# A two-layer graph kernel whose first phase goes by columns, with the diagonal block kept in SBUF and its natural tiles summed by two engines

## The chip, the cores and the metric

The kernel runs on one core of one Trainium2 chip. TensorE multiplies, VectorE and ScalarE work on tiles, GpSimd and SyncE start transfers. Time is the device time of one execution in microseconds (us). The kernel before takes 2062.57 us, the median of three runs between 2061.89 and 2065.29.

## The reference

The input `adj` is a dense 8192 x 8192 float32 matrix (268 MB), and `x` is 8192 x 128. Two graph layers follow each other, each with a product by the whole matrix:

```python
def _L0_gnn_ref(X, adj, W, b):
    adj_hat = adj + jnp.eye(adj.shape[0], dtype=adj.dtype)
    d_inv_sqrt = 1.0 / jnp.sqrt(jnp.sum(adj_hat, axis=1))
    adj_norm = adj_hat * d_inv_sqrt[:, None] * d_inv_sqrt[None, :]
    return jax.nn.relu(adj_norm @ (X @ W) + b)

def _L1_gnn_ref(x, adj, weight, self_weight):
    support = x @ weight
    output = jax.nn.relu(support + adj @ support + x @ self_weight)
    return pair_norm(output)      # over all rows
...
x = _layernorm(x + _L0_gnn_ref(x, adj, L0_gnn_W, L0_gnn_b), axis=-1)
x = _layernorm(x + _L1_gnn_ref(x, adj, L1_gnn_weight, L1_gnn_self_weight), axis=-1)
```

So the first layer needs the row sums of the matrix before it can scale anything: column block c of the product can be used only once the sums of row block c are known. The second layer needs the finished first layer in the same way.

## The kernel before

**Tiles.** The matrix is cut into 8 x 8 blocks of 1024 x 1024. A block is loaded as four tiles of 1 MB (128 partitions x 2048, two slices of 1024 columns), either transposed (`adjT`, ready for the product) or natural (`adjN`, for row sums). Four buffers `raw0` to `raw3` form a ring: SyncE's queue loads the next tile as soon as the tile four places back is consumed.

**A multiplied tile.** ScalarE rounds each slice to `hi` (L371), VectorE forms the rest `lo` (L622), and the same is done for the small factor (`rhi` L365, `rlo` L619). TensorE then makes `hi*rhi + lo*rhi + hi*rlo` for two halves of 512 columns: 6 matmuls a slice, 12 a tile (L1001). When a tile serves both layers at once it is 24, called a dual tile here. There are four buffers each for `hi` and `lo`, which is two tiles: ScalarE can start a slice only when TensorE has done the slice four back.

**Phase 1, by rows.** Row block 0 is 32 natural tiles that VectorE sums (L628). Row block k of 1 to 7 needs the sums of all its eight blocks. Its k blocks left of the diagonal come as `adjT`, are multiplied for layer 0, and their sums are made on TensorE with a matrix of ones (L1007, 4 matmuls a slice). The other 8 - k blocks come as `adjN` for VectorE. Natural tiles are put between multiplied ones as long as there are any (a "pair"), so late rows have multiplied tiles alone. There VectorE adds up three of the eight slices of a block (L718), and TensorE sums the other five. After a row `own_sums`, `lower_sums`, `degree` and `make_z` produce `zr`, the scaled factor of the next column. The phase has 256 tiles, 112 of them multiplied.

**Phase 2** walks the rows from 7 to 0: the diagonal block for layer 0, then the blocks right of it for both layers at once (dual tiles). Since rows are finished from below, layer 1 already has its factor `s1` for those columns. After each row an update of the finished row (transposes, bias, relu, layer norm, the products by `w1` and `wsum`, L774 to L813 and L1072 to L1097) is woven into the next row's tiles. Phase 2 has 144 tiles. **Phase 3** does layer 1 for the diagonal and the blocks left of it, 144 tiles. Then a tail computes the pair norm and the last layer norm and stores the result.

**Accumulators.** Layer 0 has the banks `acc0`, layer 1 the banks `acc1`. At each new row TensorE first waits until VectorE or ScalarE has read the bank, and opens it with a small product by zero (L1015).

All engines run hardware loops (`Fori`) with a register for the row. The programs of the engines are in order: an instruction that waits holds all behind it.

The lines that set the ring and the split:

```python
sp.wait_ge(slice_split, n + (o + 1 - Q) * JB)
sp.dma_start(raw[o % Q][:, :], src[k, c, q]).then_inc(loaded[o % Q], 16)
...
def pair_lo(k, i):
    for q in range(Q):
        lo_of_pair(k, i, q)
        sum_of_pair(k, i, q)
```

Of the kernel before, what the change touches and what calls it, by code (L numbers as in the profile page):

```python
# [3 lines left out]


def graph_kernel(nc, x, xT, adjT, adjN, W0, b_rows, W1, Wself, out):
# [5 lines left out]
    ds = bass.ds  # L39
# [6 lines left out]
    NB = N // BLK  # L46
    Q = 4
    JB = BLK // Q // P
    TILE = JB * BLK
    H = BLK // 512  # L50
    HALF = 512
    G = HALF // P
    EPS_LN = 1e-5
    EPS_PN = 1e-6
    assert NB >= 8 and NB % 2 == 0 and JB == 2 and H == 2

    S = Q * JB  # L60
    LOWER = NB * (NB - 1) // 2
    UPPER = NB * (NB + 1) // 2
    N2 = NB * NB * S
    N3 = N2 + UPPER * S
    SKIP = N2 - (LOWER + 1) * S

    def n1(k, c):
        return k * (NB * S) + c * S

    def n1_pair(k, i):  # L70
        return k * (NB * S) + i * (2 * S)

    def n1_rest(k, i):
        return k * ((NB - 2) * S) + i * S + 2 * NB * S

    def u1(k, c):
        return (k * (k - 1)) * (S // 2) + c * S + S

    def u1_rest(k, i):
        return (k * (k - 3)) * (S // 2) + i * S + (NB + 1) * S  # L80

    def within(v):
        return v if isinstance(v, int) else v.with_bounds(min_val=0, max_val=NB - 1)

    def phase1_rows(eng, row):

        row(1, "first")
        with eng.Fori(2, NB // 2) as k:
            row(k, "few")
        row(NB // 2, "half")  # L90
        with eng.Fori(NB // 2 + 1, NB - 1) as k:
            row(k, "many")
        row(NB - 1, "last")

    def phase1_blocks(eng, k, kind, first_pair, pair, natural, lower, after_lower=None):


        first_pair(k)
        if kind in ("few", "half", "many"):
            with eng.Fori(1, {"few": k, "half": NB // 2, "many": k * -1 + NB}[kind]) as i:  # L100
                pair(k, i)
        if kind in ("first", "few") and natural:
            with eng.Fori(k * 2, NB) as c:
                natural(k, c)
        if kind in ("many", "last"):
            with eng.Fori(0, k * 2 - NB) as i:
                lower(k, i)
            if after_lower:
                after_lower()

    def summed_on_dve(q, j):


        return j == 0 and q < Q - 1

    def n2(m, i):
        return (m * (m + 1)) * (S // 2) + i * S + N2

    def n3(m, i):
        return i * S + N3 if isinstance(m, int) and m == 0 else (m * (m - 1)) * (S // 2) + i * S + (N3 + NB * S)  # L120

# [12 lines left out]

    def k3(m):
        return NB - 1 if isinstance(m, int) and m == 0 else m - 1

    def col3(m, i):
        return i * -1 + (NB - 1) if isinstance(m, int) and m == 0 else i

    ctx = ExitStack()
    with ctx:
# [9 lines left out]


# [4 lines left out]

        raw = [sb(f"raw{q}", [P, TILE]) for q in range(Q)]

        hi = [sb(f"hi{r}", [P, BLK], f32r) for r in range(2 * JB)]
        lo = [sb(f"lo{r}", [P, BLK], f32r) for r in range(2 * JB)]


        rhi = [[sb(f"rhi{r}{l}", [P, JB * P], f32r) for l in range(2)] for r in range(2)]
        rlo = [[sb(f"rlo{r}{l}", [P, JB * P], f32r) for l in range(2)] for r in range(2)]

# [6 lines left out]
        rows = sb("rows", [P, P])  # L174
        d = sb("d", [P, N // P])
        rsum = sb("rsum", [P, NB * BLK // P])
        deg = sb("deg", [P, BLK // P])
        sq = sb("sq", [P, BLK // P])
        nw = sb("nw", [P, BLK // P])
        low = sb("low", [P, BLK // P])  # L180
        onesr = sb("onesr", [P, P], f32r)
        st = sb("st", [P, G, 6])
        ost = w0[:, 0:H * NB * 6]
        mean = sb("mean", [P, G])
        mv = sb("mv", [P, 2])
# [22 lines left out]
        ones_set = sem("ones_set")  # L208
# [4 lines left out]
        banks_free = sem("banks_free")  # L213
# [15 lines left out]
        upd_step = sem("upd_step")
# [1019 lines left out]
```

## Time and profile before

| | us |
|---|---|
| three runs | 2062.57, 2065.29, 2061.89 |
| profiled execution, first to last instruction | 2063.7 |
| TensorE busy | 1724.0 (84%) |
| VectorE busy | 1694.2 (82%) |
| ScalarE busy | 1063.7 (52%) |
| tiles loaded | 544, 570 MB |

The profiled execution is the one that the rows below come from. An engine's busy time is the time in which it executes; what lies between is idle time, with the instruction or transfer that ended it (the releaser). Matmuls overlap in the pipeline, so a single one lasts longer (0.39 us) than the distance between two of them; the distance is what counts for a sum. The page also gives the granted clock of TensorE in tenths of full speed. PEld is TensorE's weight load, which overlaps its matmuls.

### The profile page before, as it was taken

The page shows a single profiled execution, that of the slowest core. Times are in us where ns is not written, and L with a number is a line of the kernel's source. Part 1 is how long each engine was busy: PE and PEld are TensorE (multiplying, and loading weights), DVE is VectorE, ACT ScalarE, POOL GpSimd, SP SyncE. Part 2 cuts the span into 40 slices and gives each one's busy share as a digit, 9 for nine tenths or more (in the row PEclk, how much of TensorE's full clock was granted, in tenths as well). Part 3 has the DMA queues.
Part 4 walks back from the last instruction along what each step waited for, and adds up shares of the span by engine and source line. Part 5 has one row for each costly group of instructions (what it writes and reads, how often), then busy time and mean ns, then how long its engine had stood idle before and what let it go on. Part 6 is the DMA issues. An engine that isn't in the chain of part 4 may idle for free.

```text
span 2063.7 us, 26085 instructions
## 1 busy us (share of the span) xinstructions
PE 1724.0 (84%) x7538; PEld 1393.6 (68%) x7538; DVE 1694.2 (82%) x2195; ACT 1063.7 (52%) x1496; POOL 21.4 (1%) x34
## 2 busy tenths in 40 slices
PE   1134374989999997799999999999999999999993
PEld 1023263767777786677788887887887777787772
DVE  7989998999898996688675857658557999999996
ACT  0102132344545564455555545445445688888875
POOL 0000000000000100000000000000000000000001
PEclk9966787999999998899999999999999999999995
DMA  9999999999797985355555545455455699999972
GB/s 391 394 404 381 408 381 389 362 367 380 277 348 261 331 320 191 138 201 214 187 190 196 211 183 218 174 197 208 179 202 224 266 365 352 359 369 366 357 291 82
DMA packets 81956, 583.74 MB, mean 283 GB/s; under 512 B 9152, under 2 KB 9152, under 8 KB 12288
## 3 DMA queue, kind: packets, MB, share of 16 engines
q1 hardware_dynamic: 78336, 570.46, 71.7%
q0 software_dynamic: 3584, 12.85, 1.9%
q8 instruction: 17, 0.28, 0.1%
q14 instruction: 19, 0.16, 0.0%
HBM read 579.08 MB, written 4.19 MB: 283 GB/s over the span
## 4 chain that ended last, share of the span: by engine, by line
PE 60%; DVE 18%; DMA 13%; issue 5%; ACT 2%; DVEq 1%; POOL 0%; ACTq 0%; SPq 0%; POOLq 0%
PE acc L1001 54%; DVE lo L622 7%; DMA raw<-in_adjN 7%; DMA raw<-in_adjT 6%; DVE rsum L628 5%; PE acc L1007 3%; ACT hi L371 2%; DVE rlo L619 1%; PE pC L1096 1%; PE pD L1097 1%; PE acc L1015 0%; DVE t L678 0%; DVE o L898 0%; DVE s L953 0%; DMA rows<-in_b_rows 0%
## 5 line engine op out<-in xcount | busy, mean ns | idle before, releaser
L371 ACT ACTIVATE hi<-raw 128x1024 fp32r<-128x1024 f32 x800 | 821.5, 1054 | 417.8 <-DMA raw<-in_adjT 304.9
L622 DVE TENSOR_TENSOR lo<-raw,hi 128x1024 fp32r<-128x1024 f32 x800 | 943.3, 1220 | 7.1 <-ACT hi L371 7.1
L1001 PE MATMUL acc<-hi,rhi 128*128 128x512 f32 x2048 | 825.3, 403 | 122.4 <-DVE lo L622 121.5
L1001 PE MATMUL acc<-lo,rhi 128*128 128x512 f32 x2048 | 806.9, 394 | 0.0
L1001 PE MATMUL acc<-hi,rlo 128*128 128x512 f32 x2048 | 639.9, 394 | 0.0
L1001 PEld LDWEIGHTS acc<-hi,rhi 128*128 128x128 f32 x2048 | 389.8, 190 | 228.6 <-DVE lo L622 146.0
L1001 PEld LDWEIGHTS acc<-hi,rlo 128*128 128x128 f32 x2048 | 389.5, 190 | 83.8
L1001 PEld LDWEIGHTS acc<-lo,rhi 128*128 128x128 f32 x2048 | 390.1, 190 | 81.4 <-issue 3.3
L628 DVE TENSOR_REDUCE rsum<-raw 128x2048 f32 (+1 forms) x144 | 328.0, 2282 | 19.7 <-DMA raw<-in_adjN 18.5
L619 DVE TENSOR_TENSOR rlo<-zr,rhi 128x256 fp32r<-128x256 f32 x256 | 108.3, 423 | 231.3 <-ACT hi L371 229.5
L365 ACT ACTIVATE rhi<-zr 128x256 fp32r (+1 forms) x256 | 105.1, 411 | 308.5 <-PE acc L1001 297.9
L1015 PE MATMUL acc<-zero,ident 128*128 128x2 f32 x148 | 24.6, 272 | 155.4 <-ACT ux L391 124.5
L1007 PE MATMUL acc<-hi,onesr 128*128 128x512 f32 x376 | 152.1, 405 | 0.0
L1007 PE MATMUL acc<-lo,onesr 128*128 128x512 f32 x376 | 151.1, 402 | 0.0
L1015 PEld LDWEIGHTS acc<-zero,ident 128*128 128x128 f32 x148 | 23.4, 222 | 165.7 <-ACT ux L391 126.9
L619 DVE TENSOR_TENSOR rlo<-s,rhi 128x256 fp32r<-128x256 f32 x256 | 107.8, 421 | 13.2 <-ACT hi L371 11.8
L365 ACT ACTIVATE rhi<-s 128x256 fp32r (+1 forms) x256 | 102.7, 401 | 4.2 <-PE acc L1001 4.2
L1007 PEld LDWEIGHTS acc<-lo,onesr 128*128 128x128 f32 x376 | 73.1, 194 | 17.3
L1007 PEld LDWEIGHTS acc<-hi,onesr 128*128 128x128 f32 x376 | 72.5, 193 | 17.3
L376 ACT ACTIVATE sq<-deg 128x8 f32<-128x8 f32 x8 | 1.7, 209 | 126.8 <-DVE rsum L656 126.8
L718 DVE TENSOR_TENSOR o<-o,raw 128x1024 f32<-128x1024 f32 x36 | 44.1, 1225 | 2.7 <-DMA raw<-in_adjT 0.8
L813 DVE TENSOR_TENSOR o<-o,pD 128x512 f32 (+1 forms) x16 | 10.9, 682 | 26.9 <-PE pD L1097 26.9
(116 smaller groups left out, 508.2 us busy)
## 6 DMA issues: line engine op xcount, KB each, us to landing
raw<-in_adjT SPq DMA_DIRECT2D x400, 1024.0 KB, 4.9
raw<-in_adjN SPq DMA_DIRECT2D x144, 1024.0 KB, 7.4
o<-in_xT POOLq DMA_DIRECT2D x8, 512.0 KB, 8.7
s<-in_x POOLq DMA_DIRECT2D x8, 512.0 KB, 17.8
out<-zr POOLq DMA_DIRECT2D x8, 512.0 KB, 4.6
w<-in_W POOLq DMA_DIRECT2D x2, 64.0 KB, 6.1
t<-in_Wself POOLq DMA_DIRECT2D x1, 64.0 KB, 6.3
rows<-in_b_rows POOLq DMA_DIRECT2D x1, 64.0 KB, 7.0
```

What stands on the lines that cost most here:

```text
L365: nc.scalar.activation(rhi[q % 2][q // 2 if single else l][:, :], src[:, ds(c * BLK + q * JB * P, JB * P)], ACT.Copy)
L371: nc.scalar.activation(hi[q % 2 * JB + j][:, :], raw[o % Q][:, j * BLK:(j + 1) * BLK], ACT.Copy).then_inc(hi_ready, 1)
L619: V.tensor_sub(rlo[q % 2][p][:, :], src[:, ds(c * BLK + q * JB * P, JB * P)], rhi[q % 2][p][:, :].bitcast(f32))
L622: V.tensor_sub(lo[r][:, :], raw[o % Q][:, j * BLK:(j + 1) * BLK], hi[r][:, :].bitcast(f32)).then_inc(slice_split, 1)
L628: V.tensor_reduce(rsum[:, ds(c * (BLK // P) + q * JB, JB)], raw[o % Q][:, :].rearrange("p (g j) -> p g j", g=JB), AX.X, ALU.add).then_inc( ...
L718: V.tensor_add(colsum, colsum, raw[q][:, j * BLK:(j + 1) * BLK])
L813: V.tensor_add(half(o1, k, h), half(o1, k, h), pD[:, :]).then_inc(self_added, 1)
L1001: last = T.matmul(banks[h][:, :], stat[:, j * P:j * P + P], mov[:, h * HALF:(h + 1) * HALF], start=False, stop=(end and stat is rlo[q % 2] ...
L1007: last = T.matmul(acc1[h][:, :], onesr[:, :], mov[:, h * HALF:(h + 1) * HALF], start=False, stop=(end and mov is l_), skip_group_check=True)
L1015: T.matmul(bank[:, 0:2], ident[:, :], zero[:, 0:2], start=True, stop=False, skip_group_check=True)
L1096: T.matmul(pC[:, j * P:j * P + P], t2[:, j * P:j * P + P], w1[:, :], start=True, stop=True)
L1097: T.matmul(pD[:, :], wsum[:, :], t2[:, :], start=True, stop=True).then_inc(s1_made, 1)
```

## The change

The kernel is written anew around a list of tiles ("chunks") that all engines walk in the same order, without hardware loops. What is computed stays the same.

- **Phase 1 goes by columns.** Stage 0 loads the diagonal block (0,0) as `adjT` into four tiles of its own in `o1` ("keep"), and the natural tiles of row 0 right of the diagonal. Stage k of 1 to 7 multiplies column k-1: first the diagonal block (k-1,k-1) from SBUF ("cached", no transfer), then all blocks (i,k-1) below it. Beside them, one after each product tile, come the natural tiles of row k right of the diagonal and the diagonal block (k,k). No block left of the diagonal is loaded as natural, and no diagonal block as natural.
- **Sums.** Natural tiles of even q are summed on ScalarE (a copy with `accum_out`), those of odd q on VectorE (L606). The kept block is added up on VectorE into `colsum` (one `tensor_add` of two slices, then six of 128 x 1024). The sums of multiplied blocks below the diagonal are made on TensorE with `pick`, a matrix whose one column of ones puts them into row i of `pC` and `pD`. At the end of a stage `close_sums`, `read_sums`, `turn_degree` and `degree` bring the parts of one row together.
- **More work in phase 1, less after it.** Layer 0 of the diagonal blocks 0 to 6 and of block (5,6) is now done in phase 1. Phase 2 keeps (7,7), (4,5), (6,7) for layer 0, (7,7) for layer 1, and 25 dual blocks. Phase 3 has 38 blocks. The tiles loaded are 112 natural, 32 kept and 380 multiplied, 524 in all.
- **Partial results.** Each column visit to a row block ends after one block, and VectorE adds the accumulator to `ux` (L659, two of 128 x 512). Single-layer visits alternate between two sets of banks; the first matmul of a visit has `start=True`, and the small opening products are gone.

```diff
+    for k in range(NB):
+        sums, products = [], []
+        for c in range(k + 1, NB):
+            for q in range(Q):
+                sums.append(Chunk("sum", k, c, q, act=(q % 2 == 0), stage=k))
+        kept = [Chunk("keep", k, k, q, stage=k) for q in range(Q)]
+        if k == 0:
+            chunks += kept + sums
+            continue
+        sums[Q:Q] = kept
+        multiply_block(products, k - 1, k - 1, (L0,), new_visit(k - 1, (L0,), 1, [k - 1], first=(k == 1)),
+                       cached=True, stage=k)
+        for i in range(k, NB):
+            multiply_block(products, i, k - 1, (L0,), new_visit(i, (L0,), 1, [k - 1], first=(k == 1)),
+                           summed=True, stage=k)
+        if k == NB - 1:
+            multiply_block(products, 5, 6, (L0,), new_visit(5, (L0,), 1, [6]), stage=k)
+        for n, chunk in enumerate(products):
+            chunk.tail = n - (len(products) - Q)
+            chunks.append(chunk)
+            if n < len(sums):
+                chunks.append(sums[n])
...
+    add_visit(NB - 1, (L0,), 2, [NB - 1], cached=True, final=True)
+    add_visit(4, (L0,), 2, [5])
+    add_visit(6, (L0,), 2, [7], final=True)
+    add_visit(7, (L1,), 2, [7])
+    add_visit(5, (L0, L1), 2, [7], final=True)
+    add_visit(4, (L0, L1), 2, [7, 6], final=True)
+    for k in (3, 2, 1, 0):
+        add_visit(k, (L0, L1), 2, list(range(NB - 1, k, -1)), final=True)
+    add_visit(7, (L1,), 3, [6, 5, 4, 3, 2, 1, 0], last=True)
+    for k in (0, 1, 2, 3):
+        add_visit(k, (L1,), 3, list(range(k, -1, -1)), last=True)
...
+            for chunk in chunks:
+                if chunk.kind == "keep":
+                    if chunk.row > 0:
+                        sp.wait_ge(slice_split, kept_end[chunk.row - 1, chunk.q])
+                    sp.dma_start(kept[:, chunk.q * TILE:(chunk.q + 1) * TILE],
+                                 adjT[chunk.row, chunk.col, chunk.q]).then_inc(kept_in[chunk.q], 16)
+                elif chunk.ring >= 0:
+                    if chunk.ring >= RAW:
+                        by, count = ring_chunks[chunk.ring - RAW].freed
+                        sp.wait_ge(raw_free[by], count)
...
+            def sum_rows(chunk):                      # ScalarE
+                act.wait_ge(*landed(chunk))
+                for j in range(JB):
+                    g = chunk.col * BG + chunk.q * JB + j
+                    ins = S.activation(slice_of(chunk, j), slice_of(chunk, j), ACT.Copy,
+                                       accum_out=rsum[chunk.row % 2][:, g:g + 1])
+                ins.then_inc(act_summed, 1)
...
+            def add_visit_up(v):                      # VectorE
+                dve.wait_ge(slice_multiplied, v.end)
+                for h in range(H):
+                    u, a = half(ux, v.row, h), acc[v.sets[L0]][h][:, :]
+                    ins = V.tensor_copy(u, a) if v.first else V.tensor_add(u, u, a)
+                ins.then_inc(l0_read, 1)
...
+            for n, chunk in enumerate(mul_chunks):    # TensorE
+                multiply(chunk)
+                after_rows(n)
+                if chunk.stage > 0 and chunk.tail == 0:
+                    close_sums(chunk.stage)
+                if chunk.stage > 0 and chunk.tail == 1:
+                    turn_degree(chunk.stage)
+                if chunk.stage > 0 and chunk.tail == 2:
+                    first_product(chunk.stage)
```

VectorE's program in a row of pairs before (L619 and L622 split a multiplied tile, L628 sums a natural one), and then in the middle of a stage of the changed kernel (L598 and L600 split, L606 sums, L659 adds a visit to `ux`). Before:

```order
L619 ISA [waits hi_ready]
L619 TENSOR_TENSOR rlo<-zr,rhi 128x256
L622 TENSOR_TENSOR lo<-raw,hi 128x1024
L615 REGISTER_ALU
L622 TENSOR_TENSOR lo<-raw,hi 128x1024 [waits hi_ready]
L627 ISA
L628 ISA [waits loaded1]
L628 TENSOR_REDUCE rsum<-raw 128x2
L615 REGISTER_ALU
L619 ISA [waits hi_ready]
L619 TENSOR_TENSOR rlo<-zr,rhi 128x256
L622 TENSOR_TENSOR lo<-raw,hi 128x1024
```

And changed:

```order
L598 TENSOR_TENSOR rlo<-zr,rhi 128x256 [waits hi_ready]
L600 TENSOR_TENSOR lo<-raw,hi 128x1024
L600 TENSOR_TENSOR lo<-raw,hi 128x1024 [waits hi_ready]
L598 TENSOR_TENSOR rlo<-zr,rhi 128x256 [waits hi_ready]
L600 TENSOR_TENSOR lo<-raw,hi 128x1024
L600 TENSOR_TENSOR lo<-raw,hi 128x1024 [waits hi_ready]
L659 TENSOR_TENSOR ux<-ux,acc 128x512 [waits slice_multiplied]
L659 TENSOR_TENSOR ux<-ux,acc 128x512
L606 TENSOR_REDUCE s<-raw 128x2 [waits loaded3]
```

Two tiles are split for one that is summed; the other natural tile is ScalarE's, and the visit's addition stands between.

VectorE at the start of stage 7, where the stage has no natural tiles. The cached tiles of block (6,6), read from `o`, are split, and each is followed by the additions of a tile of block (7,7), which goes to the same place in `o` (L616 and L620):

```order
L598 TENSOR_TENSOR rlo<-zr,rhi 128x256 [waits hi_ready]
L600 TENSOR_TENSOR lo<-o,hi 128x1024
L600 TENSOR_TENSOR lo<-o,hi 128x1024 [waits hi_ready]
L616 TENSOR_TENSOR s<-o 128x1024 [waits sums_closed,kept_in0]
L598 TENSOR_TENSOR rlo<-zr,rhi 128x256 [waits hi_ready]
L600 TENSOR_TENSOR lo<-o,hi 128x1024
L600 TENSOR_TENSOR lo<-o,hi 128x1024 [waits hi_ready]
L659 TENSOR_TENSOR ux<-ux,acc 128x512 [waits slice_multiplied]
L659 TENSOR_TENSOR ux<-ux,acc 128x512
L620 TENSOR_TENSOR s<-s,o 128x1024 [waits col_step,kept_in1]
L620 TENSOR_TENSOR s<-s,o 128x1024 [waits col_step]
```

In the stages before, four natural tiles stand in these places and the additions come with the next four product tiles.

SyncE's queue from stage 6's kept tiles to stage 7's (L369 loads a kept tile of 1 MB, L376 a tile into the ring):

```order
L376 DMA raw<-in_adjT 128x2048 [waits act_summed]
L369 DMA o<-in_adjT 128x2048 [waits slice_split]
L376 DMA raw<-in_adjT 128x2048 [waits dve_summed]
L369 DMA o<-in_adjT 128x2048 [waits slice_split]
L376 DMA raw<-in_adjT 128x2048 [waits act_summed]
L369 DMA o<-in_adjT 128x2048 [waits slice_split]
L376 DMA raw<-in_adjT 128x2048 [waits dve_summed]
L369 DMA o<-in_adjT 128x2048 [waits slice_split]
L376 DMA raw<-in_adjT 128x2048 [waits slice_split] x4
L369 DMA o<-in_adjT 128x2048 [waits slice_split] x4
L376 DMA raw<-in_adjT 128x2048 [waits slice_split] x272
```

In stage 6 the loads of kept tiles take turns with product tiles. In stage 7 four of them follow each other, each behind the split of the tile whose place it takes, and all later tiles stand behind them.

## Rows read from the trace of the kernel before

**Rows 1.** Windows by phase: length, busy us of each engine, granted clock, DMA, GB/s.

```profile
0.00:797.50 797.50, 539.89 (x2296) 429.95 (x2296) 710.82 (x636) 276.52 (x364) 14.27 (x26) 0.90 0.90 353
797.50:1576.30 778.80, 756.59 (x3380) 616.34 (x3380) 534.03 (x910) 399.95 (x618) 0.00 (x0) 0.99 0.52 194
1576.30:2008.60 432.30, 411.86 (x1797) 335.31 (x1796) 411.37 (x509) 357.64 (x454) 0.00 (x0) 0.98 0.87 340
2008.60:2063.70 55.10, 15.67 (x66) 11.98 (x66) 37.95 (x142) 29.57 (x61) 7.08 (x8) 0.57 0.27 76
```

**Rows 2.** The page: TensorE's clock in 40 slices, and the queues that fetch instructions.

```profile
PEclk9966787999999998899999999999999999999995
...
q8 instruction: 17, 0.28, 0.1%
q14 instruction: 19, 0.16, 0.0%
```

**Rows 3.** Groups by line and shape: count, busy us, mean ns, idle before.

```profile
L622 DVE TENSOR_TENSOR lo<-raw,hi 128x1024 fp32r<-128x1024 f32 x800 | 943.3, 1220 | 7.1 <-ACT hi L371 7.1
L371 ACT ACTIVATE hi<-raw 128x1024 fp32r<-128x1024 f32 x800 | 821.5, 1054 | 417.8 <-DMA raw<-in_adjT 304.9 <-PE acc L1007 62.4 <-PE acc L1001 49.4
L628 DVE TENSOR_REDUCE rsum<-raw 128x2048 f32 x128 | 291.8, 2283 | 19.6 <-DMA raw<-in_adjN 18.5 <-issue 0.4
L718 DVE TENSOR_TENSOR o<-o,raw 128x1024 f32<-128x1024 f32 x36 | 44.1, 1225 | 2.7 <-DMA raw<-in_adjT 0.8
L1015 PE MATMUL acc<-zero,ident 128*128 128x2 f32 x148 | 24.6, 272 | 155.4 <-ACT ux L391 124.5 <-DVE t L678 11.2 <-DVE o L898 10.9
L1045 PE MATMUL acc<-o,onesr 128*128 128x512 f32 x12 | 5.6, 592 | 0.0
```

**Rows 4.** VectorE's timeline in row 0, natural tiles alone: start, length, idle before.

```profile
85.73 2.29 DVE L628 TENSOR_REDUCE rsum<-raw 128x2048 f32 x1 [0.20 <-DMA raw<-in_adjN]
```

**Rows 5.** VectorE's timeline in pairs: early in row 1, then in row 4.

```profile
100.13 0.41 DVE L619 TENSOR_TENSOR rlo<-zr,rhi 128x256 fp32r<-128x256 f32 x1
...
102.73 2.28 DVE L628 TENSOR_REDUCE rsum<-raw 128x2 f32<-128x2048 f32 x1
104.93 0.41 DVE L619 TENSOR_TENSOR rlo<-zr,rhi 128x256 fp32r<-128x256 f32 x1
```

```profile
424.45 0.43 DVE L619 TENSOR_TENSOR rlo<-zr,rhi 128x256 fp32r<-128x256 f32 x1 [0.51 <-ACT hi L371]
...
429.81 0.42 DVE L619 TENSOR_TENSOR rlo<-zr,rhi 128x256 fp32r<-128x256 f32 x1 [0.47 <-ACT hi L371]
```

**Rows 6.** The chain that ended last, TensorE: start, length, matmuls.

```profile
739.93 2.73 PE acc L1001 x12
...
755.55 2.73 PE acc L1001 x12
...
1462.04 114.30 PE acc L1001 x504
1577.71 2.84 PE acc L1001 x12
...
1863.12 65.46 PE acc L1001 x288
1930.67 77.94 PE acc L1001 x336
```

**Rows 7.** The tile raw on the load queue: time from issue to landing.

```profile
DMA to landing us min/median/max: 4.6/4.9/13.3
```

**Rows 8.** TensorE in two stretches of phase 1: busy us, granted clock, DMA, GB/s.

```profile
150.00:165.00 15.00, 0.00 (x0) 0.50 1.01 424
375.00:390.00 15.00, 14.88 (x72) 1.00 0.89 336
```

**Rows 9.** VectorE's timeline in one half of a row's update, phase 3.

```profile
1593.14 0.69 DVE L774 TENSOR_TENSOR pA<-pA,zr 128x512 f32<-128x512 f32 x1
...
1602.66 0.41 DVE L619 TENSOR_TENSOR rlo<-s,rhi 128x256 fp32r<-128x256 f32 x1
```

More of the change, by code:

```diff
@@ L30 @@
 from contextlib import ExitStack
+from dataclasses import dataclass, field
+@dataclass
+class Chunk:
+    kind: str
+    row: int
+    col: int
+    q: int
+    layers: tuple = ()
+    cached: bool = False
+    act: bool = False
+    summed: bool = False
+    stage: int = -1
+    tail: int = -1
+    ring: int = -1
+    freed: tuple = ()
+    base: int = -1
+    stats: tuple = ()
+    visit: int = -1
+@dataclass
+class Visit:
+    row: int
+    layers: tuple
+    phase: int
+    cols: list
+    final: bool = False
+    first: bool = False
+    last: bool = False
+    out: int = -1
+    end: int = -1
+    sets: dict = field(default_factory=dict)
+    waits: dict = field(default_factory=dict)
+    done: int = -1
 def graph_kernel(nc, x, xT, adjT, adjN, W0, b_rows, W1, Wself, out):
@@ L70, in n1_pair @@
[L70 to L109, printed above, removed]
@@ new lines, in graph_kernel @@
+    ORDER = {row: m for m, row in enumerate(FINAL_ROWS)}
+    done = [(c.layers[l], c.row, c.col, c.q) for c in chunks if c.kind == "mul" for l in range(len(c.layers))]
+    assert len(done) == len(set(done)) == 2 * NB * NB * Q
+    ring = slices = stats = act_sums = dve_sums = 0
+    for chunk in chunks:
+        if chunk.kind == "mul":
+            chunk.base = slices
+            slices += JB
+            chunk.stats = tuple(range(stats, stats + len(chunk.layers)))
+            stats += len(chunk.layers)
+            chunk.freed = ("split", slices)
+            visits[chunk.visit].end = slices
+        elif chunk.kind == "sum" and chunk.act:
+            act_sums += 1
+            chunk.freed = ("act", act_sums)
+        elif chunk.kind == "sum":
+            dve_sums += 1
+            chunk.freed = ("dve", dve_sums)
+        if chunk.kind != "keep" and not chunk.cached:
+            chunk.ring = ring
+            ring += 1
@@ L141, in graph_kernel, with since_last @@
+    def since_last(n):
+        for at in range(n - 1, -1, -1):
+            v = mul_chunks[at].visit
+            if last_chunk[v] == at and visits[v].last:
+                return visits[v], n - 1 - at
+        return None, -1
     ctx = ExitStack()
@@ L355, in _ @@
         def _(act):
[L356 to L372 removed]
+            S = nc.scalar
@@ L571, in _ @@
             act.wait_ge(ln_ready, 1)
-            with act.Fori(BATCH + 2, NB - 1) as k:
+            for k in range(BATCH + 2, NB - 1):
                 pair_norm(k)
@@ L578, in _ @@
             last_root(1)
-            with act.Fori(2, BATCH) as k:
+            for k in range(2, BATCH):
                 last_norm(k)
```

1103 lines of the change are left out of this document (464 added, 639 removed).

## The prediction, made before the changed kernel ran

> **What bounds the kernel now.** I read the windows by phase first, then the chain that ended last, then VectorE's timeline inside phase 1, and the groups by line for prices. The windows [rows 1] show phase 1 with 797.5 us, phase 2 with 778.8, phase 3 with 432.3 and a tail of 55.1. In phase 2 TensorE is busy for 756.6 of 778.8 us at a clock of 0.99, and VectorE and the transfers have room: it is TensorE's. The chain confirms this: 504 matmuls in 114.30 us without a break, 0.227 us each [rows 6]. So a multiplied tile costs TensorE 12 x 0.227 = 2.72 us, a dual tile 5.44, and a tile with sums (20 matmuls) 4.55. In phase 3 all three are close: TensorE 411.9, VectorE 411.4 of 432.3 us, and 24 tiles take 65.46 us, 2.73 each, in the inside of a row [rows 1, 6]. In phase 1 TensorE is busy 540 us and VectorE 711 of 797 us, transfers run at 0.90. Its early rows wait for tiles and VectorE, its late rows for TensorE: a block without natural tiles takes 755.55 - 739.93 = 15.6 us [rows 6], which is its 68 matmuls back to back. So phase 1 leaves some 250 us of TensorE idle while phase 2 has none to spare. Work moved from phase 2 into these gaps is the change's one large effect.
>
> **Prices.** VectorE's split of a tile: 102.73 - 100.13 = 2.60 us, and a natural tile 104.93 - 102.73 = 2.20, up to 2.28 [rows 3, 5]. Adding a slice of a kept tile: 1.225 [rows 3], 9.0 us for the seven of a block with their handovers. Transfers: one tile in 2.29 + 0.20 = 2.49 us where only sums are made [rows 4], and (429.81 - 424.45)/2 = 2.68 in late pairs, where VectorE waits 0.5 us for a tile [rows 5]. Half an update on VectorE: 1602.66 - 1593.14 less the one split inside, 6.9 us [rows 9]; with two additions of half a slice I take 16.5 us for a whole update. A visit's addition to `ux` is not in the trace; the nearest is an addition from a bank at 0.69 [rows 9], so 1.4 us for two; it can hardly be below 1.2 or above 1.5. TensorE's own part of an update: 756.6 us busy less 3072 products at 0.227 (697) less 30 openings at two records of 0.17 leaves 50 us for seven updates [rows 1, 3], some of it at the lower clock; I take 6.6 us each.
>
> **Stage 0.** 32 tiles as before, but eight are in flight at the start, not four, and ScalarE takes half of the sums. VectorE's 0.2 us waits per tile are for transfers [rows 4], so the rate stays at 2.49. The last tile is summed at about 85.5, then `degree`, the root, and `first_product`, which now waits for the degree. That makes `zr` ready at 91 and VectorE's first split at 92. Before it was at 95: nearly nothing gained.
>
> **Stages 1 to 6** have three parts.
> - *Four cached tiles with four natural ones, then four product tiles with the kept block.* VectorE: 8 x 2.60 + 2 x 2.28 + 9.0 + 2 x 1.4 = 37.2 us. TensorE needs 4 x 2.72 + 4 x 4.55 = 29.1, transfers 12 x 2.49 = 30. VectorE is the bound.
> - *6 - k groups of four product tiles with four natural ones.* TensorE 18.2 us, VectorE 4 x 2.60 + 2 x 2.28 + 1.4 = 16.4, transfers 8 x 2.6 = 20.8. For a tile I take 2.6 between 2.49 and 2.68, since holding times in the ring fall with VectorE's relief. The ring is full at the start of this part, which gives some 8 us of lead: 96, 75, 55, 36, 18 and 0 us for k of 1 to 6, together 280.
> - *The last four product tiles and the chain to the next `zr`.* TensorE finishes two tiles (9.1) and `close_sums`, four records of 0.47 us [rows 3], 1.9. Then `turn_degree`: 16 records, 2.5 us by the small opening products at 0.17 [rows 3]. Then a tile and `first_product` follow, 6.9 us. VectorE's chain (root, `hi` at 1.05, the split of the last tile, five small steps) is done in about the same time. Two multiplications into `zr`, `rhi` and the next `hi` follow. From the start of this part to VectorE's next split: 22.5 us.
>
> Six times 37.2 + 22.5 is 358, with 280 it is 639 us.
>
> **Stage 7** has no natural tiles, so the kept loads of (7,7) come beside the cached tiles of (6,6), into the same places. VectorE splits tile q, only then its load is issued, it lands after at least 4.6, mostly 4.9 us [rows 7], and VectorE stands before the addition with tile q+1 behind it. That is 2.6 + 4.9 + 2.45 four times over (the first with one addition), 39 us where VectorE's own work is 20.8. With 2.6 us to the first product, 18.2 for four tiles, 2 for a clock that fell meanwhile, and 18.5 for the last part: 80 us. Phase 1 ends at 92 + 639 + 80 = 811, later than before (797.5), though it does 8 blocks more, worth 8 x 4 x 2.72 = 87 us of TensorE.
>
> **Phase 2.** (7,7) and then eight single tiles carry row 7's update: VectorE 11.8 + 8 x 2.60 + 16.5 + 1.4, and TensorE ends 52.5 us after the start. Four tiles of (7,7) for layer 1 and four dual ones carry row 6's update. The single ones are paced by VectorE and the dual ones by TensorE: 49. Eight dual tiles of row 4 with row 5's update: 43.5 + 6.6 and a bank wait of 1.6, 51.7. Rows 3 to 0: 88 dual tiles 479, four updates 26.4, four bank waits 6.4, 512. The bank wait is priced by 1577.71 less 1462.04 + 114.30, 1.4 us [rows 6]. Together 665 us against 778.8: ten block products fewer are 109 of these 114 us.
>
> **Phase 3.** 152 tiles x 2.73 = 415, TensorE's part of row 0's update 6.6. That update falls on 8 single tiles instead of 12, where VectorE has 20.8 + 16.5 us, so 10 us are lost. Before, each of seven row changes cost 1930.67 - 1863.12 - 65.46 = 2.1 us [rows 6]. Now two sets of banks take turns, but VectorE has 2.8 us of extra work (two additions, two statistics) and only 0.12 us of slack per tile, so I keep 1.8. With the first bank wait of 1.6: 446 us, 14 more than before for 8 tiles more.
>
> **The tail** does the same steps; without registers and loops I take 52 for 55.1 us. **Sum:** 811 + 665 + 446 + 52 = 1974 us as the profile would count it. The profiled 2063.7 us stand 1.1 us above the median 2062.57, so 1973 us, 4.3% less.
>
> **The rivals.** (A) *The handovers in phase 1 cost more than the largest engine's work.* For: late pairs lose 0.5 us per tile pair for a tile [rows 5], and in all of phase 1 VectorE is busy only 711 of 797 us [rows 1]. If the groups run at 2.68 a tile with no lead, they take 15 x 21.4 = 321 instead of 280. With 5% on the other parts of stages 1 to 6 (18 us) the time is 2032. Against: at 100 us, with tiles in store, VectorE ran 4.80 us per pair without idling [rows 5].
>
> (B) *The engines overlap better.* The starts of the last parts hide under VectorE's lead, the lead in the ring carries over, and phase 3 loses nothing at row changes: 18 in phase 1, 10 in phase 3, some 1945 us.
>
> (C) *Fetching instructions, slower than before.* The trace shows 36 fetches in all [rows 2]. The program before lists some 6400 instructions, weight loads counted, so one fetch brings about 180; the loops then run from what is there. The straight-line program has some 14900 on TensorE alone (7457 matmuls with their weight loads), some 80 fetches. If each stops TensorE for a landing of 4.6 us [rows 7], that is 370 us: 2340. The kernel becomes slower than before from 89/80 = 1.1 us a fetch. Against it: one fetch lasts TensorE more than 20 us (90 matmuls of 0.227), and a request made that early can queue behind several tiles and still be in time. The Trainium skill, page "Runtime: NRT & Kernel Launch", section "Instruction fetch mechanics", says that the next block is fetched while the current one runs, mostly hidden, and that a taken branch out of the window stalls. By this rule the new code should not pay and the loops before should. For loops the trace shows no such price: the 504 matmuls without a break in rows 6 run through them.
>
> (D) *TensorE's clock.* With TensorE idle the clock is at 0.50 (1.2 GHz), with 14.88 of 15 us busy at 1.00 [rows 8], and phase 1 had a mean of 0.90 [rows 1]. New stages have it busier (some 600 of 720 us), so the clock should be up. Were it at 1.2 GHz for a quarter of the 400 us of stages that TensorE paces, 50 us: 2023. To become slower than before it would need almost half of them.
>
> **How the numbers follow.** Forecast 0.57, A 0.24, B 0.09, C 0.06, D 0.04. The predicted time is the forecast's, 1973. Its own bounds: visit additions, `turn_degree` and the clock after stage 7 give plus or minus 15, the lead 8, updates in phases 2 and 3 plus or minus 12. The range takes in B and most of A: 1940 to 2038. This kernel's measurement can tell about 0.2% from no change. Faster by more than that (below 2058.4) are the forecast, B, nearly all of A and half of D: 0.91. Within 0.2%, the edge of A and D: 0.03. Slower, from C and a bad D: 0.06.
>
> **What would show it.** Phase 2 should start near 811 us and run to 1476, TensorE at over 95% in its rows. In stages 1 to 6 VectorE should be without idle at the start and TensorE in the last four tiles. Stage 7 should show four waits of some 5 us before the additions to `colsum`. Stage boundaries near 248, 383, 497, 593, 671 and 731 show the terms apart. A phase 1 that ends beyond 850, TensorE idle with "issue" as the reason at even distances (C), or a clock of 0.5 within busy stages (D) would make the prediction wrong.

## The result, and the profile after

The changed kernel takes 2025.11 us (median of four runs, 2023.29 to 2030.02) against 2062.24 us for the kernel before on the same chip: a ratio of 0.982, 95% interval 0.9803 to 0.9837. It is faster, by 1.8%, where 4.3% were forecast. The time lies inside the range, but less than half of the forecast gain came.

The windows by phase of the changed kernel (columns as in [rows 1]; the first is stage 0, the second stages 1 to 7):

```profile
0.00:93.80 93.80, 11.11 (x36) 8.15 (x36) 43.68 (x33) 35.72 (x64) 4.08 (x12) 1.00 0.99 410
93.80:854.50 760.70, 679.18 (x2876) 530.37 (x2876) 591.95 (x657) 432.78 (x623) 7.04 (x11) 0.97 0.82 320
854.50:1523.60 669.10, 639.03 (x2844) 520.70 (x2844) 458.61 (x822) 329.66 (x516) 3.16 (x4) 0.98 0.51 183
1523.60:1967.60 444.00, 428.50 (x1860) 347.07 (x1860) 430.95 (x534) 373.48 (x477) 0.00 (x0) 0.99 0.91 350
1967.60:2022.30 54.70, 16.25 (x66) 12.91 (x66) 37.79 (x143) 29.57 (x61) 7.20 (x8) 0.52 0.27 77
```

| part | before [rows 1] | forecast | after |
|---|---|---|---|
| phase 1 | 797.5 | 811 | 854.5 |
| phase 2 | 778.8 | 665 | 669.1 |
| phase 3 | 432.3 | 446 | 444.0 |
| tail | 55.1 | 52 | 54.7 |
| profiled execution | 2063.7 | 1974 | 2022.3 |

43.5 us of the miss of 48 are in phase 1. To find the stage, VectorE's timeline is read at each stage's first split, the row behind the last multiplication into `zr`. Stage 1 begins with the first of these rows, phase 2 with the last:

```profile
93.85 0.43 DVE L598 TENSOR_TENSOR rlo<-zr,rhi 128x256 fp32r<-128x256 f32 x1 [1.43 <-ACT hi L439]
...
854.47 0.43 DVE L598 TENSOR_TENSOR rlo<-zr,rhi 128x256 fp32r<-128x256 f32 x1 [1.43 <-ACT hi L439]
```

| stage | 1 | 2 | 3 | 4 | 5 | 6 | 7 |
|---|---|---|---|---|---|---|---|
| forecast length, us | 155.7 | 134.7 | 114.7 | 95.7 | 77.7 | 59.7 | 80 |
| measured | 166.8 | 145.5 | 124.0 | 105.0 | 79.5 | 60.8 | 79.1 |
| over | 11.1 | 10.8 | 9.3 | 9.3 | 1.8 | 1.1 | -0.9 |

Stage 6 has no middle group and was right within 1.1 us, and stage 7 too. In stage 6 VectorE is done with the kept block at 752.27, so the first part took 37.6 us and the last 23.1. The fixed parts of a stage (37.2 and 22.5 us) were right, and what is over belongs to the middle groups. VectorE adds a visit to `ux` once in each group, so the distance between these rows is a group. From stage 1:

```profile
135.49 1.28 DVE L659 COPY ux<-acc 128x512 f32<-128x512 f32 x2
136.69 2.28 DVE L606 TENSOR_REDUCE s<-raw 128x2 f32<-128x2048 f32 x1
...
143.73 0.42 DVE L598 TENSOR_TENSOR rlo<-zr,rhi 128x256 fp32r<-128x256 f32 x1 [2.16 <-ACT hi L439]
...
155.06 0.43 DVE L598 TENSOR_TENSOR rlo<-zr,rhi 128x256 fp32r<-128x256 f32 x1 [2.27 <-ACT hi L439]
...
157.67 1.28 DVE L659 COPY ux<-acc 128x512 f32<-128x512 f32 x2
```

This group takes 22.2 us. In stages 1 to 4 ten groups can be read so, and they take 21.0 to 24.2. The last group of each stage reads shorter (18.2 to 20.0), since its visit is added when the product tiles without natural ones have begun. Over all 15 groups the stages leave 21.6 each (below). The first is no faster than the next ones. VectorE waits some 2 us for `hi` at most of the product tiles shown. At 155.06 ScalarE had a natural tile's sum ahead of it, but ScalarE's own waits are for tiles, as its timeline in the same place shows:

```profile
158.93 2.01 ACT L439 ACTIVATE hi<-raw 128x1024 fp32r<-128x1024 f32 x2 [2.65 <-DMA raw<-in_adjT]
161.46 1.06 ACT L445 ACTIVATE raw<-raw 128x1024 f32<-128x1024 f32 x1 [0.53 <-DMA raw<-in_adjN]
```

The time from issue to landing of the ring's tiles, over the whole kernel, to be set against [rows 7] (4.9); then in the groups of stage 1 (issues from 135 to 240 us); then in late pairs before (400 to 500 us):

```profile
DMA to landing us min/median/max: 4.6/6.1/20.5
```

```profile
DMA to landing us min/median/max: 5.1/7.5/10.3
```

```profile
DMA to landing us min/median/max: 5.0/6.9/8.3
```

So transfers were late, at 21.6/8 = 2.7 us a tile, though in stage 0 they come at 2.49 (a tile of 1.05 MB at 422 GB/s):

```profile
20.00:80.00 60.00, 6.55 (x20) 4.16 (x18) 27.43 (x12) 27.22 (x50) 0.00 (x0) 1.00 1.01 422
```

Two theories can explain that. **R**: the ring of four places is too short. A place is held from landing until the engine that reads the tile last is done with it, then the next transfer needs its time, and this cycle of 4 x 2.7 = 10.8 us over four places sets the rate. **M**: the memory path gives no more while three engines work. The other loss that phase 1 shows is stage 7's waits, forecast and seen.

### The profile page after: what moved, and what is told of

Same layout as the page of the kernel before. It is cut to its first block, busy times and chain, and to the rows that moved or that the text cites. A ratio compares the mean times of both kernels' runs of the same rounds, so it can differ in the third digit from the quotient of the medians.

```text
span 2022.3 us, 21035 instructions
## 1 busy us (share of the span) xinstructions
PE 1774.1 (88%) x7682; PEld 1419.2 (70%) x7682; DVE 1563.0 (77%) x2186; ACT 1201.2 (59%) x1737; POOL 21.5 (1%) x34
## 4 chain that ended last, share of the span: by engine, by line
PE 52%; DVE 28%; DMA 13%; ACT 4%; issue 2%; SPq 0%; POOL 0%; ACTq 0%; DVEq 0%
PE acc L882 15%; PE acc L884 15%; PE acc L888 15%; DVE lo L600 14%; DMA raw<-in_adjN 9%; DMA raw<-in_adjT 4%; DVE s L606 3%; DVE s L620 2%; DVE rlo L598 2%; ACT hi L439 2%; ACT raw L445 1%; PE pC L864 1%; PE pD L864 1%; DVE ux L659 1%; DMA o<-in_adjT 1%
## 5 line engine op out<-in xcount | busy, mean ns | idle before, releaser
L600 DVE TENSOR_TENSOR lo<-raw,hi 128x1024 fp32r<-128x1024 f32 x760 | 895.8, 1221 | 2.6 <-ACT hi L439 2.6
L598 DVE TENSOR_TENSOR rlo<-zr,rhi 128x256 fp32r<-128x256 f32 x256 | 108.3, 423 | 308.9 <-ACT hi L439 308.6
L433 ACT ACTIVATE rhi<-zr 128x256 fp32r<-128x256 f32 x256 | 104.5, 408 | 263.6 <-PE acc L888 227.9
L606 DVE TENSOR_REDUCE s<-raw 128x2 f32<-128x2048 f32 x56 | 127.8, 2282 | 37.5 <-DMA raw<-in_adjN 37.4
L445 ACT ACTIVATE raw<-raw 128x1024 f32<-128x1024 f32 x112 | 117.3, 1049 | 64.7 <-DMA raw<-in_adjN 64.7
L598 DVE TENSOR_TENSOR rlo<-s,rhi 128x256 fp32r<-128x256 f32 x256 | 108.2, 423 | 10.5 <-ACT hi L439 9.5
L433 ACT ACTIVATE rhi<-s 128x256 fp32r<-128x256 f32 x256 | 102.7, 401 | 6.0 <-PE acc L888 6.0
L864 PE MATMUL pC<-hi,pick 128*128 128x512 f32 x224 | 88.8, 396 | 0.0
L864 PE MATMUL pC<-lo,pick 128*128 128x512 f32 x224 | 88.0, 393 | 0.0
L864 PE MATMUL pD<-hi,pick 128*128 128x512 f32 x224 | 87.9, 392 | 0.0
L864 PE MATMUL pD<-lo,pick 128*128 128x512 f32 x224 | 87.7, 392 | 0.0
L600 DVE TENSOR_TENSOR lo<-o,hi 128x1024 fp32r<-128x1024 f32 x64 | 75.4, 1220 | 0.0
L439 ACT ACTIVATE hi<-o 128x1024 fp32r<-128x1024 f32 x64 | 64.5, 1046 | 10.4 <-PE acc L888 10.1
L620 DVE TENSOR_TENSOR s<-s,o 128x1024 f32<-128x1024 f32 x48 | 58.7, 1223 | 14.6 <-DMA o<-in_adjT 13.5
```

Of the source, the lines that this page charges most:

```text
L433: S.activation(rhi[s % DEEP][:, :], src[:, at:at + JB * P], ACT.Copy)
L439: S.activation(hi[n % DEEP][:, :], slice_of(chunk, j), ACT.Copy).then_inc(hi_ready, 1)
L445: ins = S.activation(slice_of(chunk, j), slice_of(chunk, j), ACT.Copy, accum_out=rsum[chunk.row % 2][:, g:g + 1])
L598: V.tensor_sub(rlo[s % DEEP][:, :], (zr, s1)[l][:, at:at + JB * P], rhi[s % DEEP][:, :].bitcast(f32))
L600: V.tensor_sub(lo[n % DEEP][:, :], slice_of(chunk, j), hi[n % DEEP][:, :].bitcast(f32)).then_inc(slice_split, 1)
L606: V.tensor_reduce(rsum[chunk.row % 2][:, g:g + JB], raw[chunk.ring % RAW][:, :].rearrange("p (g j) -> p g j", g=JB), AX.X, ALU.add).then_i ...
```

## The experiments

### The length of the ring

Each ring variant gives each tile of phase 1 the next of so many places; the two new places lie in `s1`, which is unused until `x` is loaded there. Phases 2 and 3 keep four.

```diff
+        part = 0 if c.stage >= 0 else 1
+        depth = RING1 if part == 0 else RAW      # RING1 = 3, 5 or 6
+        c.slot = turns[part] % depth
...
+        raw += [s1[:, (3 + 2 * r) * BLK:(5 + 2 * r) * BLK] for r in range(2)]
...
+            pool.wait_ge(slice_split, last_first)
```

> The ring of load buffers has six places in phase 1 (the two new ones lie in the part of s1 that is free until x is loaded) and four afterwards; nothing else changes. In the changed kernel a middle group of stages 1 to 5 (four product tiles, four natural tiles) takes 21.5 us where TensorE needs 18.2 and transfers at the rate of stage 0 (2.49 us a tile) 19.9. Theory R (the ring of four is too short: time from landing to release plus time from issue to landing, over four places): a group falls to about 19.9, with two more tiles in store at its start; phase 1 ends 26 to 45 us earlier and the kernel takes 1980 to 1999 us. Theory M (the memory path gives no more than one tile in 2.7 us while three engines work): a group stays at 21.5, the time from issue to landing grows by about two tiles' time (from 6 to 11 us), and the kernel stays within 5 us of 2025.

> The ring has three places in phase 1 and four afterwards. Theory R: a place is bound for some 3.3 us of holding and at least 5 to 5.5 us of transfer, so three places give one tile in 2.8 to 2.9 us: a group takes 22.5 to 23.5 us, 1 to 2 us more than with four, and the 15 groups cost 15 to 30 us; the kernel takes 2040 to 2060. Theory M: the memory path is the bound at 2.7 us a tile and one place less takes only queueing away; group 21.5 to 22, kernel 2025 to 2033.

> The ring has five places in phase 1. Measured so far, a middle group takes 23.5 to 24 us with three, 21.0 to 22.7 with four and 19.9 with six places, which is the transfers' own rate. A ring bound by cycle time (holding plus transfer) gives with five places either the rate of the transfers already (19.9 to 20.2 us, since four places' 10.8 us of cycle over five is 2.15 us a tile, less than 2.49), with one tile less in store than with six. So 1989 to 1994 us, nearly all of the gain of ring6. If instead the gain came from the store of tiles at a group's start alone, five places give half of it: 2007.

Measured: six places take 1989.31 us (ratio to before 0.9631, interval 0.9606 to 0.9655), five places 1996.56 (0.9668, 0.9652 to 0.9684), three 2080.38 in one run. The groups of stage 1, by the rows of the visits (without the last one):

| places | first group, us | later groups | kernel |
|---|---|---|---|
| 3 | 23.9 | 24.6, 23.0, 28.1 | 2080 |
| 4 | 22.2 | 21.0 to 22.7, one 23.4 | 2025 |
| 5 | 20.0 | 19.8 to 20.0 | 1997 |
| 6 | 17.6 | 19.9 | 1989 |

(Four places are the changed kernel itself.) VectorE in the kernel with six places, at the first group of stage 1:

```profile
135.63 1.28 DVE L677 COPY ux<-acc 128x512 f32<-128x512 f32 x2
...
150.59 0.43 DVE L616 TENSOR_TENSOR rlo<-zr,rhi 128x256 fp32r<-128x256 f32 x1 [1.47 <-ACT hi L457]
150.93 2.35 DVE L618 TENSOR_TENSOR lo<-s,hi 128x1024 fp32r<-128x1024 f32 x2
153.20 1.28 DVE L677 COPY ux<-acc 128x512 f32<-128x512 f32 x2
```

The later groups have 8 x 2.49 = 19.9 us with five places and with six: the rate of stage 0, with all engines at work. (In stages 2 to 4 they take up to 20.9 and 20.3.) M falls. What it said of the time from issue to landing came true all the same: in the same stretch with six places its median is 11.1 us. With 2.49 us a tile that is four to five transfers in flight, so they queue:

```profile
DMA to landing us min/median/max: 5.9/11.1/12.7
```

The trace of the changed kernel itself speaks against M too. In windows of 2 us the transfers reach the full rate with four places as well, and lose it in between:

```profile
180.00:182.00 2.00, 2.00 (x10) 1.62 (x10) 2.00 (x1) 1.49 (x2) 0.00 (x0) 1.00 1.01 426
184.00:186.00 2.00, 2.00 (x10) 1.67 (x9) 0.72 (x1) 2.00 (x6) 0.00 (x0) 1.00 0.94 311
186.00:188.00 2.00, 2.00 (x10) 1.65 (x10) 1.45 (x2) 1.77 (x3) 0.00 (x0) 1.00 0.67 217
190.00:192.00 2.00, 2.00 (x11) 1.65 (x10) 1.80 (x1) 0.00 (x0) 0.00 (x0) 1.00 1.02 426
```

The kernel with six places has no such gap there:

```profile
184.00:186.00 2.00, 2.00 (x11) 1.65 (x10) 1.92 (x3) 1.73 (x2) 0.00 (x0) 1.00 1.05 438
186.00:188.00 2.00, 2.00 (x11) 1.65 (x10) 2.00 (x2) 1.53 (x4) 0.00 (x0) 1.00 0.99 414
```

The first group shows the other half of the forecast, the lead: with six places it takes 17.6 us, faster than the transfers and near TensorE's 18.2. That tiles are in store is R's reading of it; with five there is no lead. Five places gave 28.5 of the 35.8 us that six gave, and ended 2.6 us above the expected range. With three the loss was twice what R's own figure said (55 us, not 15 to 30), since the ring then also holds up stage 0 (it ended 12.7 us later) and the product tiles beside the kept block (20.3 to 22.4 us in stages 1 to 5 instead of 18.8).

### Less holding time, same bytes

```diff
-                    S.activation(hi[n % DEEP][:, :], slice_of(chunk, j), ACT.Copy).then_inc(hi_ready, 1)
+                    wide = 256 if chunk.stage > 0 else BLK
+                    S.activation(hi[n % DEEP][:, 0:wide], slice_of(chunk, j)[:, 0:wide], ACT.Copy).then_inc(hi_ready, 1)
```

and the same for `lo` on VectorE. In stages 1 to 7 columns 256 to 1023 of `hi` and `lo` are left out, so this kernel's sums are not the reference's; its time alone is of use.

> In stages 1 to 7 the splits of slices on ScalarE and VectorE cover 256 of 1024 columns (the rest of hi and lo keeps old values, so the results of phase 1 are not those of the reference); transfers, matmuls and the order stay. This takes holding time away (a product tile is released some 2.5 us earlier) and leaves the bytes. Theory R: a middle group falls to between TensorE's 18.2 and the transfers' 19.9 us. Theory M: it stays at 21.5. In both the first part of a stage, which VectorE bounds at 37 us, falls to the transfers' 30 or TensorE's 29.

Measured: 1941.2 us in one run; the groups take 19.9 us with the ring of four. Its VectorE:

```profile
147.16 0.43 DVE L602 TENSOR_TENSOR rlo<-zr,rhi 128x256 fp32r<-128x256 f32 x1 [3.87 <-ACT hi L440]
147.50 0.75 DVE L605 TENSOR_TENSOR lo<-raw,hi 128x256 fp32r<-128x256 f32 x2
148.18 1.28 DVE L664 COPY ux<-acc 128x512 f32<-128x512 f32 x2
...
157.10 0.43 DVE L602 TENSOR_TENSOR rlo<-zr,rhi 128x256 fp32r<-128x256 f32 x1 [3.87 <-ACT hi L440]
```

VectorE now idles for 3.87 us at a time and four tiles still come only every 9.94 us: that is the transfers' rate. The same four places reach it once a product tile is held for a shorter time. That is R's second leg: what counts is holding time plus transfer over the number of places. By itself it would not refute M, since the narrow splits also take work off both engines; the longer ring, with full splits, does. The first part of a stage shrank too, as expected: stage 6 takes 53.0 us instead of 60.8.

The windows from 150 to 210 us show it in one view. First the changed kernel, then six places, then narrow splits:

```profile
150.00:210.00 60.00, 53.02 (x219) 41.39 (x218) 44.73 (x46) 39.25 (x59) 0.00 (x0) 0.97 0.98 383
```

```profile
150.00:210.00 60.00, 58.69 (x255) 47.45 (x254) 48.84 (x48) 41.35 (x61) 0.00 (x0) 1.00 1.01 422
```

```profile
150.00:210.00 60.00, 58.24 (x241) 43.97 (x240) 30.02 (x49) 25.46 (x60) 0.00 (x0) 1.00 1.01 421
```

The transfers move 383 GB/s at a busy share of 0.98 and 422 at 1.01. A busy share of 0.98 did not mean that nothing more was to be had.

### Stage 7

```diff
-        sums[Q:Q] = kept
+        sums = sums[:Q] + [None] * (Q - len(sums[:Q])) + kept + sums[Q:]
```

> In stage 7 the four kept tiles of block (7,7) stand beside the four product tiles of block (7,6) instead of beside the cached tiles of (6,6); nothing else changes. In the changed kernel stage 7 takes 79.1 us and VectorE waits there four times for 3.7 to 5.0 us for a kept tile, 18.4 in all. If those waits are what the order of stage 7 costs, they vanish: stage 7 takes about 61 us, the kernel about 2007. Rival: TensorE bounds the part that follows (18.2 us for four product tiles, then the last part), and VectorE's nine us of additions move beside it, so that less than 10 us are won.

In the changed kernel VectorE waits as the prediction said. The additions of the four kept tiles:

```profile
783.06 1.23 DVE L616 TENSOR_TENSOR s<-o 128x1024 f32<-128x1024 f32 x1 [4.96 <-DMA o<-in_adjT]
...
791.83 2.48 DVE L620 TENSOR_TENSOR s<-s,o 128x1024 f32<-128x1024 f32 x2 [3.74 <-DMA o<-in_adjT]
...
801.85 2.48 DVE L620 TENSOR_TENSOR s<-s,o 128x1024 f32<-128x1024 f32 x2 [4.93 <-DMA o<-in_adjT]
...
811.72 2.48 DVE L620 TENSOR_TENSOR s<-s,o 128x1024 f32<-128x1024 f32 x2 [4.78 <-DMA o<-in_adjT]
```

With the kept tiles one block later (VectorE, stage 7):

```profile
789.92 2.35 DVE L600 TENSOR_TENSOR lo<-raw,hi 128x1024 fp32r<-128x1024 f32 x2
792.19 1.22 DVE L616 TENSOR_TENSOR s<-o 128x1024 f32<-128x1024 f32 x1
793.33 0.42 DVE L598 TENSOR_TENSOR rlo<-zr,rhi 128x256 fp32r<-128x256 f32 x1
```

Measured: 1999.39 us (0.9676, interval 0.9655 to 0.9696), 26 us less; stage 7 takes 51.2 instead of 79.1 us, 28 less where 18 were expected. Not the waits alone go (18.4 us): the additions (9 us) move beside tiles that TensorE paces, which fits the rest. The rival said that this would take from the gain; it adds to it.

### Block (5,6)

```diff
-        if k == NB - 1:
-            multiply_block(products, 5, 6, (L0,), new_visit(5, (L0,), 1, [6]), stage=k)
...
+    add_visit(5, (L0,), 2, [6])
     add_visit(4, (L0,), 2, [5])
```

> The changed kernel, with block (5,6) of layer 0 multiplied in phase 2 before block (4,5) instead of at the end of stage 7. If stage 7 had idle time for it, phase 1 would stay and phase 2 would grow by 11 to 12 us: 2036. By the trace these four tiles stand at the end of stage 7 where TensorE has just done four tiles with sums back to back, so they are paid for where they stand: stage 7 shrinks by 4 x 2.72 = 11 us less the longer tiles with sums that now hide nothing else, phase 2 grows by 11 to 12: 2025 plus or minus 3.

Measured: 2023.89 us (0.9812, interval 0.9789 to 0.9835), the same as the changed kernel. Stage 7 shrinks by 14.7 us (79.1 to 64.4), and in the profiled execution what follows phase 1 grows by 10.5. (That execution is the shortest of its four; stage 4 came out 3.9 us shorter in it, of which more below.) A tile moved into phase 1 gains only where TensorE waits for something else; at the end of stage 7 it does not.

### Who sums the natural tiles

```diff
-                sums.append(Chunk("sum", k, c, q, act=(q % 2 == 0), stage=k))
+                sums.append(Chunk("sum", k, c, q, act=(q != 3), stage=k))    # fourth
+                sums.append(Chunk("sum", k, c, q, act=(False), stage=k))     # alldve
```

> The changed kernel, with every fourth natural tile (q = 3) summed on VectorE instead of every second; ScalarE takes three of four. Theory V: the first part of each stage 1 to 6 is bound by VectorE (37.2 us), so it loses one sum of 2.28 us there: 35.0 us, and the middle groups, bound by the ring of four, stay at 21.5. That is 6 x 2.2 = 13 us less: 2012. Rival: ScalarE's sum of one tile stands ahead of the next tile's hi in its program, tiles are held longer, and the groups grow by 0.5 to 1 us each, 8 to 15 us in all: 2020 to 2027, no gain.

> The changed kernel, with all natural tiles summed on VectorE, as in the kernel before. Theory V: the first part of stages 1 to 6 grows by 4.6 us to 41.8, and a middle group has 4 x 2.60 + 4 x 2.28 + 1.3 = 20.8 us of VectorE's work beside a ring of four, so that it grows from 21.5 to 22.5 or 23: 28 + 15 to 22 = 43 to 50 us more, 2068 to 2075. Rival: VectorE's waits in the groups (2 to 4 us for each two tiles) absorb it and only the first parts grow: 2053.

Measured: every fourth on VectorE 2020.75 us (0.9784, interval 0.9769 to 0.9799), 4 us less than the changed kernel (7 by the ratios, 0.9784 against 0.982) and not 13. Stages 1 to 6 take 168.6, 144.8, 123.7, 100.8, 79.6 and 60.7: the same but for stages 1 and 4, and stage 4's difference need not be the sums'. It takes 105.0 us in the changed kernel, but 102.7 and 101.1 in the two runs that changed only stage 7. All on VectorE: 2047.35 in one run, 22 us more and not 43 to 50. Stage 6, which has no middle group, grows by 2.7 us where 4.6 were expected for a first part. Six times 2.7 is 16 of the 25 us that the six stages grow by, which leaves 0.6 us for each of the 15 groups where 1 to 1.5 were expected; those that can be read take 21.2 to 22.6. Both expectations failed on the first part of a stage, which is not VectorE's alone, and the second on the groups too.

### Together

> The ring of six in phase 1 and the kept tiles of stage 7 beside block (7,6), together. Alone they gave 36 and 26 us. They work in different stages (1 to 5, and 7), so they should add: 2025 - 36 - 26 = 1963 us, between 1958 and 1968. Rival: the gain of the ring is partly a gain of stage 7 (its transfers too), so that the sum is 10 us short.

> As both, and every fourth natural tile summed on VectorE. With the ring of six a middle group is bound by the transfers (19.9 us) and the first part of a stage by VectorE. So 2.2 us are won in each of six first parts, 13 us: 1950. Rival: as soon as VectorE is relieved the first part is bound by something else, TensorE (29.1) being the next in size but ScalarE's order (hi, sum, hi) possibly before it: 0 to 5 us won.

Measured: both together 1958.28 us (median of five, ratio 0.9486, interval 0.9473 to 0.9499), 5.1% less than before and the fastest version. The two gains add as expected. With every fourth tile on VectorE besides, 1962.75 (0.95, 0.9482 to 0.9518): no gain. VectorE at the start of stage 2 shows why. First with both together:

```profile
253.41 0.43 DVE L616 TENSOR_TENSOR rlo<-zr,rhi 128x256 fp32r<-128x256 f32 x1 [1.59 <-ACT hi L457]
...
257.22 2.27 DVE L624 TENSOR_REDUCE s<-raw 128x2 f32<-128x2048 f32 x1
...
262.02 0.42 DVE L616 TENSOR_TENSOR rlo<-zr,rhi 128x256 fp32r<-128x256 f32 x1
```

And with every fourth tile on VectorE:

```profile
254.02 0.43 DVE L616 TENSOR_TENSOR rlo<-zr,rhi 128x256 fp32r<-128x256 f32 x1 [1.59 <-ACT hi L457]
...
258.30 0.43 DVE L616 TENSOR_TENSOR rlo<-zr,rhi 128x256 fp32r<-128x256 f32 x1 [0.39 <-ACT hi L457]
258.64 2.35 DVE L618 TENSOR_TENSOR lo<-o,hi 128x1024 fp32r<-128x1024 f32 x2
262.58 0.42 DVE L616 TENSOR_TENSOR rlo<-zr,rhi 128x256 fp32r<-128x256 f32 x1 [1.58 <-ACT hi L457]
```

ScalarE has, for a cached tile and the sum behind it, `rhi`, two slices of `hi` and two of the sum, 4.4 us in all (in the changed kernel's timeline from 151.48 to 155.88). It works on in order, so the `hi` of the next tile comes after that, and VectorE waits 1.6 us behind each sum of ScalarE's. The first such wait stands in both kernels. The sum taken from VectorE (2.2 us) comes back as the two others, 0.39 and 1.58: from the stage's first split to the first addition of the kept block both kernels take 20.3 us.

## Why the prediction was right and wrong

**Right.** Phase 2 (665 forecast, 669.1), phase 3 (446, 444.0), stage 0 (92, 93.8), the fixed parts of a stage (59.7; stage 6 took 60.8) and stage 7 (80, 79.1) with its four waits. The account of the gain stands: phase 2 lost 109.7 us, and ten block products fewer had been put at 109. Its single parts were not compared with their forecasts.

**Wrong: the middle groups.** The sentence "for a tile I take 2.6 between 2.49 and 2.68, since holding times in the ring fall with VectorE's relief" and the next, "the ring is full at the start of this part, which gives some 8 us of lead", made 280 us of 15 groups. Measured are 323 (the stages less 59.7 each, 681.6 - 358.2 = 323.4). These 43 us are the miss, and both steps failed. The larger is the lead: 15 groups at 20.8 are 312, so 32 us were taken off for tiles in store, and no first group of stages 1 to 4 showed any. The other is the rate: 21.6 us a group instead of 20.8, 11 us in all. The mechanism was there as rival A, and its price for the groups, 321, was right to 3 us, with 2.68 a tile and no lead; its further 5% on the other parts were not there. Two facts were mis-read. First, for a product tile the holding time did not fall. It is held while ScalarE makes `hi` and VectorE splits it, and VectorE's relief leaves that as it is. Before (ScalarE and VectorE at one tile in row 4) it lasts from 423.25, where the wait for the tile ends, to 424.80 + 2.35 = 427.15, which is 3.9 us:

```profile
423.25 2.01 ACT L371 ACTIVATE hi<-raw 128x1024 fp32r<-128x1024 f32 x2 [3.08 <-DMA raw<-in_adjT]
...
424.80 2.35 DVE L622 TENSOR_TENSOR lo<-raw,hi 128x1024 fp32r<-128x1024 f32 x2
```

In the changed kernel from 149.00 to 152.78, 3.8 us:

```profile
149.00 2.00 ACT L439 ACTIVATE hi<-raw 128x1024 fp32r<-128x1024 f32 x2 [4.04 <-DMA raw<-in_adjT]
...
150.43 2.35 DVE L600 TENSOR_TENSOR lo<-raw,hi 128x1024 fp32r<-128x1024 f32 x2
```

Natural tiles were indeed held for less, by the trace's landings 3.7 us before and 2.2 now (medians of the two stretches above). That did not make tiles come faster: the median time from issue to landing grew from 6.9 to 7.5 us instead. Second, being full gives no lead if the ring is only just long enough: a tile is replaced only when it is consumed, and with four places its replacement was not there when its turn came. The runs show the lead with six places (17.6 us for the first group in stage 1), not with five (20.0). Why four places lose the full rate in gaps, though 3.8 us of holding and the 4.9 of a landing [rows 7] over four places would be only 2.2 us a tile, no run tested. ScalarE and VectorE free places unevenly (in the changed kernel tiles are issued at 161.17, 163.77, 164.15 and 167.73), which would leave few transfers in flight at times.

The kernel with six places comes out near the forecast, in part by luck: stages 1 to 5 take 154.6, 136.2, 116.3, 97.5 and 79.3 us where 155.7, 134.7, 114.7, 95.7 and 77.7 stood, and phase 1 ends at 818.1 instead of 811. Its 15 groups take 286.5 us where 280 stood, but in another way: later groups at 19.9 and not 20.8, and 12 us of lead (15 x 19.9 = 298.5) and not 32.

**Right in sum, wrong in its reason: the first part of a stage.** 37.2 us was worked out from VectorE alone, 37.6 measured. The runs with other shares of the sums show that ScalarE's order paces its first tiles nearly as much, so that VectorE's relief changes nothing.

**Wrong and small: the tail.** 52 us were taken for want of loops, 54.7 measured against 55.1 before.

**The other rivals.** C, fetching: the changed kernel makes 103 fetches.

```profile
q8 instruction: 60, 0.98, 0.2%
q14 instruction: 43, 0.35, 0.0%
```

TensorE still runs at 0.227 us a matmul in phase 2 (six from one of these rows to the next, 1.36 us), whose time was within 4 us of the forecast, so they cost nothing that shows.

```profile
1420.86 0.45 PE acc L888 x2
1422.22 0.45 PE acc L888 x2
```

This agrees with the rule of the Trainium skill, page "Runtime: NRT & Kernel Launch", section "Instruction fetch mechanics", that the next block is fetched while the current one runs. D, the clock: 0.97 in stages 1 to 7 against 0.90 in phase 1 before. Neither shows a part in the miss. B did not occur.

## What to carry to other kernels

A ring of load buffers has a rate of its own: places over (holding time plus the time from issue to landing). Compare that with the transfers' rate before giving the stage to any engine, and take both times from a stretch of the same kind. With the landing time of a quiet stretch the sum is too kind: it gave 2.2 us a tile for the four places that ran at 2.7. Here a fifth place reached the transfers' rate and a sixth gave a store for the start of the groups. Where several engines work in turn on a tile, taking work from one helps only if no other stands ahead of it in the same order; and a kept buffer that is refilled right behind its last reader, with its consumer next in line, costs most of a landing each time (3.7 to 5.0 us here).

## What the runs showed of the hardware

Transfers kept 2.49 us for a tile of 1 MB (422 GB/s) with TensorE at 58.7 of 60 us, VectorE at 48.8 and ScalarE at 41.4, the same as with sums alone in stage 0; I had left room for contention, and this stretch shows none. The busy share of the transfer engines read 0.98 at 383 GB/s and 1.01 at 422, so it tells little of what is left. An activation with an accumulated sum takes 1.04 to 1.06 us for 128 x 1024, and its accumulator read another 0.19, half of which overlaps: two slices with their reads take 2.10 us (151.48 to 153.58), two of `hi` 1.92 (153.96 to 155.88).
